# Attention pooling by diagonal blocks and side sums in a one-core adaLN and FFN kernel

## The reference, cut to what matters

```
attn_in = tanh(hidden @ W1 + b1)             # per batch: 512 x 128
scores = attn_in @ v                         # one score per key: 512
mask = l <= j  (kind 0),  l >= j  (kind 1),  l != j  (kind 2)
p = softmax(where(mask, scores[l], -1e30))   # 512 queries j x 512 keys l
pooled = (p @ hidden) / count(mask)          # 512 x 512
h = bitlinear(pooled, w1, b1)                # rmsnorm, int8 by row, product
```

## Time and profile before

| what | value |
|---|---|
| median of 3 runs | 885.37 us (883.66 to 886.49) |
| the profiled execution, its own time | 881.29 us |
| its span | 879.5 us |
| TensorE busy, share of the span | 768.5 us, 87% |
| VectorE, ScalarE, GpSimd busy | 532.7, 490.1, 339.6 us |
| mean granted TensorE clock | 0.942 |

### The profile page before, as it was taken

The page is one execution under the profiler, slowest core; times in us unless marked ns, Lnnn a source line. Parts: engine busy times, 40 slices in busy tenths (PEclk is TensorE's granted clock), DMA queues, the critical chain, the costliest instruction groups (busy, mean ns, idle before and its releaser), DMA issues. The chain is left out here.

```text
span 879.5 us, 10973 instructions
## 1 busy us (share of the span) xinstructions
PE 768.5 (87%) x3828; PEld 495.0 (56%) x3828; DVE 532.7 (61%) x1029; ACT 490.1 (56%) x682; POOL 339.6 (39%) x330
## 2 busy tenths in 40 slices
PE   5774799998999999634999999975799999999997
PEld 3321277776777777412777777764355555555553
DVE  2672445454455455214465565543799999999995
ACT  1110226664377778414566556632687777777783
POOL 0486413243142122204444444420254555444553
PEclk9987789999999999856999999987899999999999
DMA  6999427897295486331111102000012221222212
GB/s 203 347 414 334 146 107 273 288 318 239 97 257 130 131 229 145 43 131 48 49 49 49 40 19 88 1 1 10 27 49 72 73 69 64 68 65 73 72 62 82
DMA packets 42534, 109.07 MB, mean 124 GB/s; under 512 B 4208, under 2 KB 4992, under 8 KB 39280
## 3 DMA queue, kind: packets, MB, share of 16 engines
q1 hardware_dynamic: 35616, 94.71, 30.4%
q0 software_dynamic: 6352, 13.06, 8.0%
q10 hardware_dynamic: 512, 0.61, 0.2%
HBM read 88.63 MB, written 28.13 MB: 133 GB/s over the span
## 5 line engine op out<-in xcount | busy, mean ns | idle before, releaser
L1297 PE MATMUL ps<-ff_q,qt 128*128 128x512 bf16 x512 | 123.8, 387 | 7.1 <-DVE h L1362 6.3
L1323 PE MATMUL ps<-ff_q,ht 128*128 128x512 bf16 x512 | 115.7, 379 | 2.4 <-DVE ht L1379 2.4
L824 PE MATMUL ps<-w_h,inner_l 128*128 128x512 f32 x256 | 102.8, 401 | 3.6 <-DVE inner_l L773 3.6
L1283 POOL TENSOR_SCALAR hb<-h 128x2048 bf16<-128x2048 int8 x32 | 60.8, 1900 | 111.2 <-ACT h L1341 111.2
L639 POOL DMA_INDIRECT x_after_experts<-y,row_of_slot x32 | 51.4, 1605 | 134.7 <-DVE y L759 127.4
L826 PE MATMUL ps<-w_h,inner_h 128*128 128x512 f32 x256 | 101.2, 395 | 0.0
L825 PE MATMUL ps<-w_l,inner_h 128*128 128x512 f32 x256 | 101.1, 395 | 0.0
L1341 ACT ACTIVATE h<-h,to_q 128x2048 int8<-128x2048 f32 x32 | 64.1, 2002 | 44.3 <-DVE to_q L1393 44.3
L1362 DVE SCALAR_TENSOR_TENSOR h<-ps,scale,bias 128x1024 f32<-128x1024 f32 x64 | 81.6, 1279 | 9.3 <-PE ps L1297 9.3
L773 DVE SCALAR_TENSOR_TENSOR inner_l<-ps,inner_h 128x512 fp32r<-128x512 f32 x64 | 44.2, 691 | 69.9 <-ACT inner_h L708 69.4
L1297 PEld LDWEIGHTS ps<-ff_q,qt 128*128 128x128 bf16 x512 | 49.4, 99 | 64.0 <-DVE h L1362 7.5
(11 more groups left out here) (211 smaller groups left out, 1516.1 us busy)
## 6 DMA issues: line engine op xcount, KB each, us to landing
w_in_sb<-in_w_in_t SPq DMA_DIRECT2D x8, 2048.0 KB, 12.7
w_raw<-in_w_out_t SPq DMA_DIRECT2D x16, 1024.0 KB, 5.5
raw<-in_ff_t SPq DMA_DIRECT2D x16, 1024.0 KB, 7.6
xt<-in_x_t SPq DMA_DIRECT2D x8, 1024.0 KB, 9.3
x_after_experts<-in_x SPq DMA_DIRECT2D x8, 1024.0 KB, 16.8
x_sum<-x_after_experts SPq DMA_DIRECT2D x8, 1024.0 KB, 4.8
x<-x_after_experts SPq DMA_DIRECT2D x32, 256.0 KB, 2.7
out<-res SPq DMA_DIRECT2D x32, 256.0 KB, 2.0
```

What stands on the lines that cost most here:

```text
L824: pe.matmul(ps[:, s, :], inner_l[:, k % 2, c], w_h[:, k % RING, :], start=k == 0, stop=False)
L1297: m = pe.matmul(ps[:, f, :], qt[:, t, k, :], ff1_q[:, k, f * 512:(f + 1) * 512], start=k == 0, stop=k == KD - 1)
L1323: m = pe.matmul(ps[:, OUT[t3 % 2], :], ht[:, k, :], ff2_q[:, k, :], start=k == 0, stop=k == KF - 1)
```

## The change

Queries and keys are split into 4 blocks of 128. Only the block of keys that has the query's own number is still weighed key by key (`prob`, now 128 keys x 512 queries, one 128-column piece for each block, and the mask of 128 x 128 is the same for each). Of the other blocks a query sees either all keys or none. There are 8 sides: for each block, all blocks ahead of it and all blocks behind it. For each side, exp(score - running maximum) of its keys is computed once (`side_key`, 128 x 4 x 8) and TensorE makes the sums over keys of these weights times x (`side_sum`) and of the weights alone (`side_den`), in `side_sums`. A query then takes its sides by one more product, with `side_pr`, a matrix of 80 rows by 512 queries that holds exp(running maximum - top) where the mask allows it (rows 0 to 7 and 8 to 15 high x high and high x low parts, and so on, in groups of 32).

- TensorE: `pool_block` has four wide and three narrow products in place of twelve and eight; `side_sums(b2)` (8 wide, 4 narrow, 48 rows) stands first in the loop; `pool_block(b2, 1)` moves ahead of the score product; all four `turn_q` tiles stand together between `pool_block(b2, 2)` and `(b2, 3)`.
- ScalarE: copies `side_sum` and `side_den` out first in the loop; after `square(b2, 1)` an exponential of `side_key`, four of 128 columns of `prob`, one of `side_prob`, and two rounded copies.
- GpSimd: casts the int8 rows to bf16 (`qb`) between the halves of `x_l`; then two subtractions, `prob` and `side_prob`. `q8` and `qb` have two buffers.
- VectorE: loses the cast `qb`; gets the low parts of the sums, the small operations on `side_max`, `side_key` and `side_top`, the split of `side_key`, and has two low parts in place of four. `keep_q` of all four tiles stands behind them.
- SyncE: `bias1` comes after the second `x_sum`. The mask table has 640 columns in place of 896.

```diff
 GpSimd
+    pool.tensor_tensor(x_l half 0)
+    if half == 0 and inside(b3, BATCH):
+        pool.wait_ge(q8_ready, TPB * (b3 + 1))
+        pool.tensor_scalar(qb[:, b3 % 2, :, :], q8[:, b3 % 2, :, :], 1.0, 0.0, ALU.mult, ALU.add).then_inc(qb_ready, 1)
+    pool.tensor_tensor(x_l half 1)
+    pool.wait_ge(top_ready, b1 + 1)
+    pool.tensor_tensor(prob, mask[:, kd, 0:P] broadcast, top, ALU.subtract).then_inc(own_arg, 1)
+    pool.tensor_tensor(side_prob, mask[0:SIDE_ROWS, kd, P:P + SEQ], top[0:SIDE_ROWS], ALU.subtract).then_inc(side_arg, 1)
 TensorE
+def side_sums(b):
+    pe.wait_ge(side_key_cp, 2 * (b + 1))
+    pe.wait_ge(x_l_cp, 2 * (b + 1))
+    pe.wait_ge(scanned, b + 1)
+    for l in range(TPB):
+        lhs = side_key_r[:, l, 0:SUM_ROWS]
+        pe.matmul(ps[0:SUM_ROWS, ATT_BANK, :], lhs, x_l[:, b % 2, l, :], start=l == 0, stop=False)
+        pe.matmul(ps[0:SUM_ROWS, ATT_BANK, :], lhs, x_h[:, b % 2, l, :], start=False, stop=l == TPB - 1)
+    if b >= 1:
+        pe.wait_ge(small, N_SMALL * (b - 1) + 1)
+    for l in range(TPB):
+        m = pe.matmul(ps[0:SUM_ROWS, DEN_BANK, SIDE_DEN], side_key_r[:, l, 0:SUM_ROWS], one_col[:],
+                      start=l == 0, stop=l == TPB - 1)
+    m.then_inc(sum_mm, 1)
 pool_block(b, j)
-    for l in range(TPB):   # 3 wide and 2 narrow products each
+    pe.matmul(num, prob_l[q], x_h[:, b % 2, j, :], start=True, stop=False)
+    pe.matmul(num, prob_h[q], x_l[:, b % 2, j, :], start=False, stop=False)
+    pe.matmul(num, prob_h[q], x_h[:, b % 2, j, :], start=False, stop=False)
+    pe.matmul(num, side_pr[q], side_sum[:], start=False, stop=True)
+    pe.matmul(den, prob_l[q], one_col[:], start=True, stop=False)
+    pe.matmul(den, prob_h[q], one_col[:], start=False, stop=False)
+    pe.matmul(den, side_pr[q], side_den[:], start=False, stop=True).then_inc(pooled, 1)
 turn_q(b, ts)
-            if t >= 2:
+            if TPB * b + t >= 2:
                 pe.wait_ge(q_cp, TPB * b + t - 1)
 ScalarE, after square(b2, 1)
+    act.wait_ge(key_arg, b1 + 1)
+    act.activation(side_key[:], side_key[:], ACT.Exp).then_inc(key_exp, 1)
+    act.wait_ge(own_arg, b1 + 1)
+    for c in range(TPB):
+        q = prob[:, c * P:(c + 1) * P]
+        act.activation(q, q, ACT.Exp, bias=key_score[:, b1 % 2, c:c + 1]).then_inc(own_exp, 1)
+    act.wait_ge(side_arg, b1 + 1)
+    act.wait_ge(side_top_ready, b1 + 1)
+    act.activation(side_prob[:], side_prob[:], ACT.Exp, bias=side_top[0:SIDE_ROWS, 0:1]).then_inc(side_exp, 1)
...
+    act.activation(prob_h[:, b1 % 2, :], prob[:], ACT.Copy).then_inc(prob_h_cp, 1)
...
+    act.activation(side_pr[:, b1 % 2, :], side_prob[:], ACT.Copy).then_inc(side_h_cp, 1)
 VectorE, end of the loop
                         if inside(b2, BATCH):
                             greatest(b2, 0)
                             greatest(b2, 1)
-                        if inside(b3, BATCH):
-                            keep_q(b3, (0, 1))
-                        if inside(b1, BATCH):
-                            low_part(b1, (0, 1))
-                        if inside(b3, BATCH):
-                            keep_q(b3, (2, 3))
+                        if inside(b1, BATCH):
+                            split_side_keys(b1)
+                            ve.wait_ge(prob_h_cp, b1 + 1)
+                            ve.tensor_tensor(prob_l[:, b1 % 2, :], prob[:], prob_h[:, b1 % 2, :].bitcast(F32), ALU.subtract)
+                            ve.wait_ge(side_h_cp, b1 + 1)
+                            ve.tensor_tensor(side_pr[low_rows, b1 % 2, :], ..., ALU.subtract).then_inc(side_l_cp, 1)
+                        if inside(b3, BATCH):
+                            keep_q(b3, range(TPB))
                         if inside(b2, BATCH):
                             greatest(b2, 2)
-                        if inside(b1, BATCH):
-                            low_part(b1, (2, 3))
```

More of the change, by code:

```diff
@@ L68, in constant_table @@
         "ident": p == np.arange(P)[None],
+        "key_side": spread(np.where(np.stack([[[l < c for c in range(TPB)], [l > c for c in range(TPB)]] for l in range(TPB)]),
+                                    0.0, MASKED).reshape(1, TPB * SIDES)),
+        "row_side": p % SIDES == np.arange(SIDES)[None],
         "count": np.concatenate([j + 1, SEQ - j, np.full((P, TPB), SEQ - 1)], 1),
@@ L78, in mask_table @@
 def mask_table():
-    p, d = np.arange(P)[:, None], np.arange(MASK_W)[None] - (TPB - 1) * P
-    seen = [p <= d, p >= d, p != d]
-    return np.stack([np.where(s, 0.0, MASKED) for s in seen], 1).astype(mybir.dt.np(BF16))
+    p, d, j = np.arange(P)[:, None], np.arange(P)[None], np.arange(SEQ)[None]
+    own = [p <= d, p >= d, p != d]
+    side, chunk = p % SIDES // TPB, p % TPB
+    row = (p % 32 < 2 * SIDES) & (p < SIDE_ROWS) & (j // P == chunk)
+    sides = [row & (side == 0), row & (side == 1), row]
+    return np.stack([np.where(np.concatenate(s, 1), 0.0, MASKED) for s in zip(own, sides)], 1).astype(mybir.dt.np(BF16))
 def inside(i, n):
@@ L954, in _ @@
                             for half in (0, 1):
                                 ts = slice(2 * half, 2 * half + 2)
[L956 to L965, removed]
+                                pool.tensor_tensor(x_l[:, b1 % 2, ts, :], x_sum[b1 % 2][:, ts, :],
+                                                   x_h[:, b1 % 2, ts, :].bitcast(F32), ALU.subtract).then_inc(x_l_cp, 1)
@@ new lines, in _ @@
+                            if b1 >= 1:
+                                pool.wait_ge(prob_l_cp, b1)
+                                pool.wait_ge(side_l_cp, b1)
+                            pool.tensor_tensor(
+                                prob[:].rearrange("p (c q) -> p c q", c=TPB), mask[:, bass.ds(kd, 1), 0:P].broadcast_to([P, TPB, P]),
+                                top[:].rearrange("p (c q) -> p c q", c=TPB), ALU.subtract).then_inc(own_arg, 1)
+                            pool.tensor_tensor(
+                                side_prob[:].unsqueeze(1), mask[0:SIDE_ROWS, bass.ds(kd, 1), P:P + SEQ],
+                                top[0:SIDE_ROWS, :].unsqueeze(1), ALU.subtract).then_inc(side_arg, 1)
+                        elif inside(b3, BATCH):
+                            pool.wait_ge(q8_ready, TPB * (b3 + 1))
+                            pool.wait_ge(q_tr, TPB * (b3 - 1))
+                            pool.tensor_scalar(qb[:, b3 % 2, :, :], q8[:, b3 % 2, :, :], 1.0, 0.0,
+                                               ALU.mult, ALU.add).then_inc(qb_ready, 1)
```

202 lines of the change are left out of this document (119 added, 83 removed).

## The result

The changed kernel takes 912.07 us (median of 4 runs, 909.40 to 913.92) where the kernel before takes 884.51 (4 runs, 883.03 to 886.49): a ratio of 1.0308, 95% interval 1.0273 to 1.0342. It is slower by 27.6 us. The forecast was 912, made of a median of 885.37 for the kernel before, which a fourth run has since moved to 884.51, and a change of 26.5 us.

What follows compares the result with a forecast made beforehand. Bound: a four-engine loop level with TensorE. Period 27.4 + 1.0 + 1.6 = 30.0 us; 37.7 - 7.0 - 5.0 + 0.8 = +26.5 on 881.3 gives 907.8 profiled, 912 us median; range 893 to 930.

Steps and rivals of the forecast that it cites:

- What bounds the kernel: Edited stage: a loop over four engines closes at nearly the same time as TensorE's work, period 23.72 us.
- The path of one full iteration: From pooling block 3's end through side sums, GpSimd's row, keep_q and block 3 again: 27.4 us in place of 23.72.
- The clock: TensorE's clock drops after idle stretches, so block 3 and side sums run slower: 0 to 2.8 us, taken 1.6.
- The holds: VectorE's maximum and tiny key operations held by GpSimd's current instruction: 0 to 2.5 us a period, taken 1.0.
- Rival 3: VectorE's small operations are held by GpSimd each time: period 32, +39 us, 924 us; chance 0.16.
- Sum of the full iterations: Six full iterations (4th to 9th), each 6.3 us longer than 23.72: +37.7 us.
- Beginning: First iterations, before the full ones: shorter pooling brings the zero point to 428.4 in place of 435.4, -7.0 us.
- Drain: The drain's pooling iteration goes from 24 us to some 19: -5 us.
- Last cast: The last cast is on GpSimd, 1.90 us for a shorter one: bounds 0 and 1.9, taken +0.8.
- Rival 1: TensorE's clock stays up: period 28.4, +17 us, 902 us; chance 0.13.
- Rival 2: Faster: the loop's detour through keep_q and TensorE costs nothing; period 22.3 us, -20 us, 866 us; chance 0.09.
- Rival 4: TensorE was the one bound and everything else follows: period 16.3, -56 us, 829 us; chance 0.03.

Runs made afterwards that it cites:

- e8: Changed kernel with keep_q of tiles 0 and 1 early, int8 cast on VectorE, one-SBUF-operand small operations, GpSimd's mask subtractions ahead of x_l's second half: 862.80 us.
- e7: Changed kernel plus 17 and 37 dummy products in TensorE's two idle stretches, to keep its clock up: 897.59 us, ratio 1.0154.
- e5: Changed kernel with VectorE's small operations on the sides given at most one SBUF operand, the other in PSUM: 905.80 us, ratio 1.0245.
- e1: Changed kernel with keep_q of turned tiles 0 and 1 moved ahead of the greatest values and both low parts on VectorE: 895.91 us, ratio 1.0139.
- e2: Changed kernel with TensorE's pooling block 3 moved right behind block 2, ahead of the four turns: 900.62 us, ratio 1.0187.
- e3: Changed kernel with the cast of the int8 rows moved from GpSimd back to VectorE: 904.24 us, ratio 1.0225.
- e9: Changed kernel with GpSimd making the int8 cast twice, the second into a tile nobody reads: 916.61 us, ratio 1.0380.
- e4: Changed kernel plus 12 dummy TensorE products ahead of the wait for the cast and 28 ahead of the third turn: 907.59 us, ratio 1.0274.
- e11: Against e8: 13 dummy TensorE products added ahead of the first turn and 4 ahead of the side sums: 866.11 us, ratio 0.9814.

## Why the prediction was right

- *What bounds the kernel*: a loop over four engines, level with TensorE. Shown by e8 and the changed kernel together: with the same work on TensorE the period is 22.33 or 30.02 us, by the order and the waits.
- *The path of one full iteration*: forecast 27.4 at full pace without holds; e7, with the clock up and the holds in it, has 27.61, and 27.0 with the 0.6 of the holds (e5) taken off, so the base was some 0.4 us too long. Most of that is the side sums, taken at 2.3 us and 2.03 at full clock in e7. (The quantizing step, 4.4 + 3.64 - 0.40, gives 7.6 and not 7.9; some 0.2 of the difference is the hand-over to ScalarE, which the text leaves out. Measured: 8.27.) The steps up to GpSimd's last subtraction are each within 0.6 us. keep_q's place is the step that matters (e1: 2.7 us; e2: 2.0).
- *The clock*, taken at 1.6 of 0 to 2.8 us: 2.2 in the iteration shown, 2.4 by e7. The mechanism is right. The size taken was too small: block 3 and four of the eight wide side sums paid in full, a fifth in part, and the turns, which the forecast left out, paid 0.25.
- *The holds*, taken at 1.0 of 0 to 2.5 us: the mechanism is there in full (0.19 for 2.29 us), but its price is 0.60 us by e5 (0.35 over all six iterations). I sized its end at 1 to 2 us behind the row; the chain ends with GpSimd's own last instruction, 0.2 us behind it, and ScalarE is at the other exponentials until then. Too large by 0.4 or more, which with the base's 0.4 made up for the clock's 0.8. That the three cancel to give 30.0 is luck; the path itself is not. Rival 3 had the mechanism right and the price wrong.
- *Sum of the full iterations*: 6 x 6.3 = 37.7 forecast; from the side sums of the first full iteration at 431.84 to those of the drain at 612.53 there are 180.7 us in place of 142.3, +38.4. *Beginning*: the first full iteration starts 41.5 us behind the first transposes in place of 47.9, -6.4 (forecast -7.0). *Drain*: 612.5 to 632.2, 19.7 in place of 24.1, -4.4 (forecast -5). *Last cast*: 12.2 in place of 11.3, +0.9 (forecast +0.8). Together +28.5, forecast +26.5. That the median was hit all the same is luck of another kind: by the medians the change is 27.6, and the kernel before has 884.51 in place of 885.37.
- *Rival 1* (the clock stays up) is out by the profile; e7 shows what it would have given, 897.6. *Rival 2* was a matter of the detour, and e8 shows that it can be taken away: the forecast for it, 22.3 us a period and 866 us, is close to e8's 22.33 and 862.8, but e8 needed three edits besides keep_q's place, and its loop closes through VectorE's denominators, so that the agreement is in part chance. *Rival 4*: TensorE was not the one bound.
- What the prediction did not see is that VectorE's queue and the exponentials behind GpSimd's row end within half a microsecond of each other (0.26 us in the iteration shown), so that taking away either alone gives less than its length (e3, e5, e9).

## What to carry to other kernels

When an engine is made 7 us lighter in a loop where a chain over the other engines is as long as it, walk the chain through the new order before counting the gain; here two copies of 0.4 us in the wrong place of one queue cost 16 us. Work moved to GpSimd is paid a second time by VectorE's small operations with two SBUF operands, and putting one of them in PSUM takes that away; here it was worth 0.4 to 0.6 us a period, and 2.7 us together with the cast's move. Two waits that end together must be taken away together, so an edit that gives little alone (e3, e5) isn't proof that its wait is harmless.

## What the runs showed of the hardware that was not expected

- TensorE's clock fell in 2.3 us without a product, behind 5.5 us of uninterrupted ones (e4), and in e11 with no idle stretch longer than 0.84 us in the 5 us before it. The prediction had only seen it fall behind 3.96 and 5.48 us.
- A VectorE copy of 32 constants from SBUF to PSUM took 0.18 us while GpSimd's cast ran (e5), and a cast of 64 elements from SBUF to SBUF took 1.71 us while its x_l ran. Both have one input; they differ in where the output lies and in its type. Type alone does not make the hold: the copy of 8 float32 elements from SBUF to float32 in SBUF (L1272) took 1.79 us in the changed kernel. Its input is strided, and the two were not separated further.
- Dummy products that compute nothing made the kernel 14.5 us faster (e7), more than taking the int8 cast off GpSimd (7.8).
